# Two deformable convolutions on one core: five of nine taps gathered instead of seven, four built densely from rows of hat functions

## What is computed

```python
# stage 1 (b = 0 in the kernel); stage 2 (b = 1) is the same without mask and norms
out  = relu(group_norm(conv1x1(x, w1)))                 # 64 channels
om   = conv3x3(out, w_off) + b_off                      # 27 maps: 9 x, 9 y, 9 masks
mask = sigmoid(om[:, 18:])
px, py = own_x + kx + om[:, :9], own_y + ky + om[:, 9:18]
sampled = bilinear_sample(out, py, px) * mask           # 4 corners, zero outside the image
out  = relu(group_norm(einsum('bckhw,ock->bohw', sampled, w2)))
out  = relu(group_norm(conv1x1(out, w3)) + x)
```

## Time and profile before

| | |
|---|---|
| median of 3 runs | 269.4 us (268.47 to 271.7) |
| the profiled execution | 269.83 us |
| its span | 268.0 us |
| PE busy | 210.7 us, 79% |
| DVE busy | 158.3 us, 59% |
| ACT busy | 117.9 us, 44% |
| POOL busy | 136.0 us, 51% |
| mean granted TensorE clock | 0.877 |

### The profile page before, as it was taken

The page is one execution under the profiler, slowest core; times in us unless marked ns, Lnnn a source line. Parts: engine busy times, 40 slices in busy tenths (PEclk is TensorE's granted clock), DMA queues, the critical chain, the costliest instruction groups (busy, mean ns, idle before and its releaser), DMA issues. The chain is left out here.

```text
span 268.0 us, 2403 instructions
## 1 busy us (share of the span) xinstructions
PE 210.7 (79%) x808; PEld 109.6 (41%) x808; DVE 158.3 (59%) x270; ACT 117.9 (44%) x159; POOL 136.0 (51%) x127
## 2 busy tenths in 40 slices
PE   8999987787979568196997979489876764999920
PEld 7364963543333223034873746233332231343500
DVE  2965537766867954844166466567476676352271
ACT  2120335786686837001206148848738551023231
POOL 6000017877878877870010077788777787720010
PEclk9999995678899999677799975979899998699965
DMA  7400113323233232230000223223323223310004
GB/s 257 171 0 2 39 41 98 98 86 93 80 99 93 83 98 80 79 98 21 0 2 0 78 66 110 78 83 95 98 78 97 81 80 97 100 39 0 0 0 157
DMA packets 8654, 19.80 MB, mean 74 GB/s; under 512 B 1985, under 2 KB 4162, under 8 KB 8514
## 3 DMA queue, kind: packets, MB, share of 16 engines
q0 software_dynamic: 5376, 14.69, 18.0%
q1 hardware_dynamic: 3122, 4.44, 4.8%
q10 hardware_dynamic: 144, 0.52, 0.5%
HBM read 17.55 MB, written 2.10 MB: 73 GB/s over the span
## 5 line engine op out<-in xcount | busy, mean ns | idle before, releaser
L321 POOL DMA_INDIRECT G<-table,idx x112 | 129.1, 1153 | 58.1 <-issue 47.7
L558 DVE TENSOR_TENSOR GW<-G,corner_w 128x1024 f32<-128x1024 f32 (+1 forms) x32 | 34.9, 1091 | 52.0 <-DMA G<-table,idx 51.1
L951 PE MATMUL ps<-first,GS 128*128 128x128 f32 x64 | 15.5, 328 | 37.1 <-DVE GS L573 37.0
L753 ACT ACTIVATE sT<-ps 128x256 f32<-128x256 f32 x32 | 12.2, 381 | 64.0 <-PE ps L951 64.0
L906 PE MATMUL ps<-x,V 128*64 128x512 f32 x64 | 38.4, 731 | 0.0
L723 ACT ACTIVATE near_y<-ps,dbias 128x1024 f32<-128x1024 f32 x32 | 35.4, 1106 | 1.5 <-PE ps L898 1.5
L308 POOL TENSOR_TENSOR rstd<-var,half_neg 64x1 f32<-64x1 f32 (+1 forms) x4 | 2.6, 638 | 64.0 <-DVE var L371 42.2
L726 ACT ACTIVATE hat_y<-near_y 128x1024 f32<-128x1024 f32 x32 | 33.8, 1057 | 1.0
L799 PE MATMUL ps<-first 128*128 128x128 f32 x180 | 28.6, 316 | 0.0
L799 PEld LDWEIGHTS ps<-first 128*128 128x128 f32 x180 | 25.7, 224 | 4.2 <-issue 3.9
L951 PEld LDWEIGHTS ps<-first,GS 128*128 128x128 f32 x64 | 7.1, 153 | 45.0 <-DVE GS L573 43.7
(11 more groups left out here) (132 smaller groups left out, 235.1 us busy)
## 6 DMA issues: line engine op xcount, KB each, us to landing
G<-table,idx POOLq DMA_INDIRECT x112, 2.9
second<-in_second SPq DMA_DIRECT2D x1, 1552.5 KB, 8.6
table<-feat_t SPq DMA_DIRECT2D x4, 256.0 KB, 2.3
out<-x SPq DMA_DIRECT2D x4, 256.0 KB, 2.2
x<-in_x ACTq DMA_DIRECT2D x1, 512.0 KB, 4.6
x<-in_x SPq DMA_DIRECT2D x1, 512.0 KB, 5.4
first<-in_first SPq DMA_DIRECT2D x1, 224.0 KB, 4.4
at_w<-in_w_b SPq DMA_DIRECT2D x1, 1.0 KB
```

Of the source, the lines that this page charges most:

```text
L321: pool.indirect_dma_start(out=G[:, done % RING, k, :], out_offset=None, in_=table[b], in_offset=bass.IndirectOffsetOnAxis(ap=idx[b][:, n:n ...
L558: dve.tensor_tensor(GW[:, :, k0:k1].rearrange("p c k e -> p k c e"), G[:, (b * TILES + t) % RING, k0:k1].rearrange("p k (c e) -> p k c e", ...
L753: act.activation(sT[:, t % 2, 2 * part:2 * part + 2], ps[:, B_ST[part], 0:2 * P] .rearrange("p (q n) -> p q n", n=P), ACT.Copy).then_inc(s ...
L951: mm = pe.transpose(ps[:, B_ST[part], q % 2 * P:(q % 2 + 1) * P], GS[:, t % 2, k:k + 2, :].rearrange("p k e -> p (k e)"), ident)
```

## The change

Five taps are gathered, and four are dense. Of these, taps 5 and 6 are built by products as before, taps 7 and 8 by squares, since hy * hx = ((hy + hx)^2 - hy^2 - hx^2) / 2.

- **Rows of hats instead of full hats.** `fill(name)` spreads offsets of four groups of 32 rows at once (names Y, XA, XB, C, D and, for the modulation, MY and MS): each partition group holds a distance to 32 rows or columns of the image. ScalarE takes |distance| and the hat once for each. `duo` holds a hat as its f32r high part in one group and the low remainder in the next; it is made from `signed` (ScalarE, times 1 or -1) and VectorE's `high_and_low`. The own position and the bias come with the offset convolution: a tenth matmul with four rows, `aux`.
- **Spreads.** For each of 16 chunks `spread_product` multiplies one half of `duo["Y"]` (64 rows) by a one-hot matrix in f32r into banks B_P (4, 5): the y hat of 128 source pixels. VectorE multiplies it by hat_x. `spread_square` does so with all 128 rows of C or D into banks B_S (6, 7), which gives hy + hx; ScalarE squares it. Both banks are single: a spread waits until the one before is read.
- **Main matmuls.** `add_pair(c)` adds the square's matmul on partitions 64 to 127 of B_C1 and the product's on 0 to 63, in turns for both halves of the image. V holds four taps. `correct()` subtracts the squares of the single hats; `merge()` adds the upper 64 rows, which ScalarE copies to SBUF, to the lower ones.
- **Gathers.** 40 a stage instead of 56; G holds four tiles instead of five. GW, GA, GS, the transposes (three pairs, one of them with a zero weight half) and the contraction are no longer in two parts. Offsets come to pixels by matmuls with `pick`, which also adds high and low parts; L481's additions are gone.
- **Moved.** POOL fills `sums` from the constants; ScalarE makes `spread` from `eye` right after `first` has landed; `second` has 3409 columns instead of 3105. The residual and `last_conv3(0, ...)` of stage 2 stand behind the loop. `hidden_stats(0)` stands behind it too.

```diff
-DENSE = 2
-GTAPS = TAPS - DENSE
-PARTS = [(0, 4), (4, GTAPS)]
-BESIDE = [0, 0, 1, 1, 2, 1, 1, 2, 1, 1, 2, 1, 1, 2, 0, 0]
-RING = 5
+GTAPS = 5
+PAIRS = GTAPS // 2 + 1
+PROD = 2
+SQUARE = 2
+LATE_TILE = 2
+CORRECT_AT = 6
+RING = 4
+PRING = 3
+SRING = 2
...
+            def samples(b):                                  # ScalarE
+                distance(b, "Y")
+                hat_of(b, "Y")
+                if b == 0:
+                    modulation("MY")
+                pixel_hats(b)
+                distance(b, "XA")
+                hat_of(b, "XA")
+                sign_rows(b, "Y")
+                distance(b, "C")
+                hat_of(b, "C")
+                if b == 0:
+                    modulation("MS")
+                distance(b, "XB")
+                hat_of(b, "XB")
+                sign_rows(b, "C")
+                for t in range(TILES):
+                    if t == LATE_TILE:
+                        distance(b, "D")
+                        hat_of(b, "D")
+                    square(b, 2 * t)
+                    square(b, 2 * t + 1)
+                    if t == LATE_TILE:
+                        sign_rows(b, "D")
+                    if t == CORRECT_AT - 1:
+                        hat_squares(b, 0)
+                        hat_squares(b, 1)
+                    if t:
+                        to_contract(b, t - 1)
...
                     for k in range(TAPS):
-                        om = pe.matmul(ps[:, B_OFF + h, :],
+                        om = pe.matmul(ps[0:2 * SLOT, B_OFF + h, :],
...
+                    pe.matmul(ps[0:2 * SLOT, B_OFF + h, :], offw[b][HID:HID + 4, TAPS].rearrange("p s o -> p (s o)"),
+                              half(aux, h), start=False, stop=True).then_inc(s_omc, 1)
...
+                def spread_product(c):
+                    i, t = divmod(c, TILES)
+                    done = b * PROD_CHUNKS + c
+                    rows = slice(i * HID, (i + 1) * HID)
+                    if c == 0:
+                        pe.wait_ge(s_duo, b * len(HATS) + 1)
+                        pe.wait_ge(s_readp, fills_p(b, P_FILLS[b][-1]) + 1)
+                    if done:
+                        pe.wait_ge(s_prod, done)
+                    for h in range(2):
+                        mm = pe.matmul(ps[:, B_P + h, :], spread[rows, i, t], half(duo["Y"], h)[rows],
+                                       start=True, stop=True)
+                    mm.then_inc(s_bp, 1)
+
+                def spread_square(c):
+                    i, t = divmod(c, TILES)
+                    name = "CD"[i]
+                    if t == 0:
+                        pe.wait_ge(s_duo, b * len(HATS) + HATS.index(name) + 1)
+                        pe.wait_ge(s_reads, fills_s(b, "XB") + 1)
...
+                        pe.matmul(ps[:, B_S + h, :], spread[:, i, t], half(duo[name], h),
+                                  start=True, stop=True).then_inc(s_bs, 1)
+
+                def add_pair(c):
+                    i, t = divmod(c, TILES)
+                    pe.wait_ge(s_prod, b * PROD_CHUNKS + c + 1)
+                    pe.wait_ge(s_sq, 2 * (b * SQUARE_CHUNKS + c + 1))
+                    for h in range(2):
+                        mm = pe.matmul(ps[HID:P, B_C1 + h, :], V[:, t, PROD + i, :], half(SS[c % SRING], h),
+                                       start=(c == 0), stop=(c == SQUARE_CHUNKS - 1))
+                        mm.then_inc(s_up if c == SQUARE_CHUNKS - 1 else s_mains, 1)
+                        mm = pe.matmul(ps[0:HID, B_C1 + h, :], V[:, t, i, :],
+                                       half(SP[(b * PROD_CHUNKS + c) % PRING], h), start=(c == 0), stop=False)
+                    mm.then_inc(s_mainp, 1)
...
+                for u in range(TILES):
+                    if u == LATE_TILE:
+                        pe.wait_ge(s_sq, 4 * (b * TILES + u))
+                        fill("D")
+                    if u == CORRECT_AT:
+                        correct()
+                    spread_product(2 * u)
+                    spread_square(2 * u)
+                    if u:
+                        add_pair(2 * u - 1)
+                    if u >= 1:
+                        turn(u - 1)
+                    if u >= 2:
+                        contract(u - 2)
+                    spread_product(2 * u + 1)
+                    spread_square(2 * u + 1)
+                    add_pair(2 * u)
+                add_pair(SQUARE_CHUNKS - 1)
+                if b:
+                    residual(x2, QUARTERS)
+                contract(TILES - 2)
+                turn(TILES - 1)
+                merge()
+                contract(TILES - 1)
                 if b:
                     last_conv3(0, 1)
                     last_conv3(0, 0)
-                contract(UNITS - 1)
```

More of the change, by code:

```diff
@@ L79 @@
 B_V = 0
-B_D = [4, 5]
-B_Y = 6
+B_P = 4
+B_S = 6
 B_C3 = 4
+CW_AT = 3 * P
 def width(fields):
@@ L120, in conv_chain @@
         split = sb("split", [P, PW, PW], F32R)
-        offw = [sb(f"offw{b}", [P, TAPS, 4, SLOT], F32R) for b in range(2)]
+        offw = [sb(f"offw{b}", [P, TAPS + 1, 2, SLOT], F32R) for b in range(2)]
+        aux_own = sb("aux", [P, N], F32R)
+        aux = aux_own[HID:HID + 4]
         om_sb = sb("om_sb", [2 * SLOT, N])
@@ L173, in conv_chain @@
         pg = sb("pg", [P, TILES, 2 * D])
-        th = sb("th", [2 * D, N])
+        th = near[1][0:2 * D]
         mt = sb("mt", [D, D])
@@ L640, in _ @@
             act.activation(warm[:], zeros[0:H, 0:1], ACT.Sigmoid)
+            act.wait_ge(s_first, 16)
+            for side in range(2):
+                rows = slice(side * HID, (side + 1) * HID)
+                for variant in range(2):
+                    place = spread[rows, variant].rearrange("p t (r x) -> p (t r) x", x=W)
+                    eye = fld["eye"][rows]
+                    act.activation(place, (eye[:, None, :] if side != variant else eye[:, :, None])
+                                   .to_broadcast([HID, H, W]), ACT.Copy).then_inc(s_spread, 1)
             act.wait_ge(s_const, 1)
@@ new lines, in fill @@
+                def fill(name):
+                    for h in range(2):
+                        if name in P_FILLS[b]:
+                            bank, filled = B_P, s_fillp
+                            pe.wait_ge(s_readp, fills_p(b, name)) if fills_p(b, name) else None
+                        else:
+                            bank, filled = B_S, s_fills
+                            pe.wait_ge(s_reads, fills_s(b, name)) if fills_s(b, name) else None
+                        mm = pe.matmul(ps[:, bank + h, :], sel[:, TILE_NAMES.index(name), :], half(om_split, h),
+                                       start=True, stop=True)
+                    mm.then_inc(filled, 1)
@@ new lines, in correct, with merge @@
+                def correct():
+                    pe.wait_ge(s_cw, SQUARE * b + SQUARE)
+                    pe.wait_ge(s_hatsq, SQUARE * b + SQUARE)
+                    for h in range(2):
+                        for i, name in enumerate("CD"):
+                            pe.matmul(ps[i * HID:(i + 1) * HID, B_C1 + h, :], CW[:, i],
+                                      half(full[FULL[name]], h), start=False, stop=False)
+                def merge():
+                    for h in range(2):
+                        pe.wait_ge(s_upper, 2 * b + h + 1)
+                        mm = pe.matmul(ps[0:HID, B_C1 + h, :], ident[0:HID, 0:HID], half(upper, h),
+                                       start=False, stop=not h)
+                        if not h:
+                            mm.then_inc(s_c2[b + 1], 1)
@@ new lines, in deform @@
+                fill("Y")
+                if b == 0:
+                    fill("MY")
+                taps_of_pixels(1)
+                fill("XA")
+                fill("C")
+                if b == 0:
+                    pe.wait_ge(s_sums, 4)
+                    pe.wait_ge(s_sig, 2)
+                pe.wait_ge(s_VD, b + 1)
+                for t in range(TILES):
+                    mm = pe.matmul(ps[:, B_SMALL, CW_AT:CW_AT + SQUARE * HID],
+                                   sums[:, t].rearrange("p g j -> p (g j)"),
+                                   V[:, t, PROD:].rearrange("p d e -> p (d e)"),
+                                   start=(t == 0), stop=(t == TILES - 1))
```

659 lines of the change are left out of this document (344 added, 315 removed).

## The result

The changed kernel takes 285.53 us (median of 4, 284.88 to 287.08), the kernel before 269.08 us beside it: a ratio of 1.06, 95% interval 1.0516 to 1.0684. It is slower, as forecast; 294 us was 8.5 us too much. The profiled execution took 287.08 us with a span of 285.3 us, 17.3 us more than the 268.0 of before.

The account below looks back on a forecast made before the run. Gathers on POOL bound the kernel before; TensorE and the setup would bound the new one. Span 268.0 + 10.8 (block 0) + 10.9 (block 1) + 2.1 (end) = 291.8, plus 1.8: 294 us, range 266 to 342.

Parts of the forecast that it names:

- POOL waiting for GW: In the loop: POOL idle, waiting for GW, was listed among the signs that would show the prediction right.
- if records start in program order: Main pairs on TensorE: only upper 2 with lower 1 can share a slot, so eight records take five slots, 2.13 us.
- A tile without the pairs: TensorE's spreads, transposes, contraction and shape changes in one loop tile: 4.25 us.
- full-overlap rival: Main pairs: both column halves fully side by side, a tile 7.7 us, the time 280 us; chance 0.15.
- the first case: Main pairs staggered, two halves partly side by side: a tile 8.3 to 9.4 us, 290 to 308 us; chance 0.45.
- Changes of shape: TensorE, where the used array shape changes: the next weights aren't hidden, 0.2 us more.
- the faster rival: Loop: halves fully side by side and shape changes free, a tile 6.3 us, 258 us in all; chance 0.12.
- T: TensorE's time for one tile of the new loop; 8.5 us was taken, between 7.7 and 11.1.
- the prediction's own terms: Block 0's loop: clock 2.0, eight tiles, fill D and its distance 1.1, correct() 2.1, contraction to last contraction 3.5 us.
- the four of the prediction: Loop start: 1.2 GHz, 2 us of work done in about 4 us, +2.0 us a block.
- the last step: Setup, VectorE's high_and_low C before the loop's first square spread: 1.3 us, a product's 1.22 and the hand-over.
- the taken case: Main pairs at five slots, a tile 8.5 us: 294 us, own interval 288 to 308.

Follow-up runs that it names:

- the repeated execution: The changed kernel, unedited, profiled a second time: 278.46 us (span 276.7), beside 270.91 for the kernel before, one execution each.
- the grouped kernel: The changed kernel with a pair's four matmuls in the order upper, upper, lower, lower instead of upper, lower, upper, lower: 281.17 us.

## Why the prediction was right, and where it was wrong

**The sign, and the bound.** Right: POOL no longer paces the loop. In stage 1 its last gather ends at 100.9 us, 31 us ahead of the loop's end, VectorE never waits for a gather (51 us of such waits in the earlier trace rows), and TensorE is 98% busy in loop 0. The sign "POOL waiting for GW" itself hardly showed: never in the repeated execution, three times and 8.5 us in all in the profiled one, all in stage 2 behind a late signal. Five gathers a tile would have let the kernel be 23 us a block faster; TensorE's own sum, 8 x 7.67 = 61 us from a start at 61 to 63, is why it isn't. Taking away two more gathers changed 0.1 us.

**The step that failed: "if records start in program order".** A tile without the pairs was to cost 4.25 us, and measured 7.67 - 2 x 1.71 = 4.25. The pair was to cost five slots, 2.13 us; it costs four, 1.71. That makes 16 x 2 x 0.42 = 13.4 us too much in the sum. The full-overlap rival had 0.15 of the chance, "against: it needs records to leave program order", and they do. The Trainium skill, "TensorEngine Tiling (Array Packing)", Key Properties, has it right that different tiles load weights and multiply in parallel: 0.01 us between the two starts. The same skill's "TensorE: Matmul & The Clock Gate", in its Part 3 on packing small matmuls, says that matmuls start and end strictly in the order of the program, without reordering; the grouped kernel differs, 92.35 before 92.81, and the measurement decides. The weight loads of both halves also lie side by side (0.14 us each, 0.01 apart), so the 308 us end of the first case had no ground either.

**Changes of shape.** Right: 0.2 forecast, 0.22 measured, also between 64 and 128 rows, so the faster rival was excluded for the reason given.

**The loops.** With T = 7.67, the prediction's own terms give 2.0 + 61.3 + 1.1 + 1.7 + 3.5 = 69.6 us for block 0 and 73.2 for block 1. The repeated execution has 69.8 and 73.1. That the single terms are right doesn't follow. The low clock lasted 7.5 us and not the four of the prediction, a loss of 3.7 on paper; that its removal was worth 1.4 to 2.7 less 0.7, near the 2.0 of the sum, is luck. And the wait ahead of `correct()`, 1.06 us, had no term, so another term is too large by about as much; no run shows which.

**The setup.** ScalarE's way from the first distance to the last sign was to take 14.8 us and took 62.01 - 46.97 = 15.0, the last step 1.3 and took 1.4. But the first distance was to start at 43.9 and started at 46.97 (44.87 in the repeated execution). The Y fill stands behind the 8 matmuls of the V taps, which run at the low clock: 3.76 us in the profiled execution, 2.97 in the repeated one. I had moved it by 0.75 from L893's start instead of adding up what was put ahead of it. What I charged at nothing, the constants' work ahead of the features, was nearly that in stage 1: ScalarE's first feature activation starts at 28.77 in the kernel before, at 28.96 in the repeated execution, and at 29.82 in the profiled one, where the difference isn't explained.

**The end.** The first projection, L1130, starts 262.43 - 259.67 = 2.8 us behind the last contraction's start, L968 started 0.5 behind the earlier trace rows: 2.3 us later, 2.1 forecast. Not foreseen: the span ends 3.2 us behind the last instruction of ScalarE in every kernel of this shape (285.3 - 282.1), and 5.8 in the kernel before (268.0 - 262.2). That gives 2.6 us back; no run here says why.

**The whole.** For the repeated execution: loop 0 ends at 131.1 instead of 126.0 (+5.1), loop 1 at 251.65 instead of 242.8 (+8.85, of which 3.7 in stage 2), the projections +2.3, the end -2.6: 8.6 us, and 276.7 - 268.0 is 8.7. The full-overlap rival said 280 us, and 278.5 was measured. The other 8.6 us of the profiled execution are 2.4 in stage 2's setup and 4.2 in its loop, both with late signals, and 2.1 ahead of stage 1's loop (0.9 of them ahead of the features, the rest in matmuls at the lower clock); the loop 0 of that execution gives 1.2 back, what lies between the blocks takes 1.3. A cause for the late signals stood in none of the cases. The range held the time because it reached down to 266 for the other rivals. The 285.5 us lie in no case's own interval, between full overlap (to 284) and the taken case (from 288), and that they are within 9 us of 294 is luck: the pair's fifth slot made the forecast too long, and the late signals, which it doesn't have, made the kernel longer. Against the 278.5 us without them it is 15 us off.

## What to carry to other kernels

Two f32 matmuls on the two column halves of the array cost what one costs here, in both orders that were tried: count such a pair once, but count each change of the used shape at about 0.2 us. When an engine is unloaded, add up the next engine's stream first: here 23 us a block of gathers were bought off, and TensorE's 7.7 us a tile, with a setup that no longer runs beside the loop, took more than that. And a kernel's executions should be read singly before an effect is claimed: edits that took 6 us out of a loop could be seen in the loop's own length and not in any median.

## What the runs showed of the hardware

- A matmul of one column half starts beside one of the other half that stands up to four records ahead of it (92.35 beside 92.33). Eight records in 1.71 us against 3.41 on one half; over the kernel 278.5 against 336.4 us.
- A change of the used shape between 64 and 128 rows costs 0.22 us (steps of 1.33 and 1.11), as one between 128 rows and 1 did (0.2).
- TensorE can nearly stop: single matmuls 1.40 us apart instead of nearly eight a microsecond, for 2 to 17 us, beginning at a granted clock of 1.00 where that was read, in nine of thirteen profiled executions of the changed kernel and its variants, and in none of the kernel before. Its matmuls are already recorded as started while those who wait for them stand. In the profiled execution this is at most some 6.6 us of 17.3. It appeared only beside gathers' traffic or up to 2.0 us behind it, which many executions have without it. Its cause is open.
- 7.5 us at a granted clock of 0.50 at a loop's start, on paper 3.7 us lost, were worth 1.4 to 2.7 us in the loop when the clock was kept at 1.00, and the loop started 0.7 us later; a part of the rest is a wait for ScalarE (0.50 us at 63.94) that came in their place.
